# Transposing the normalised activations with DMAs in place of TensorE

## The chip, the cores and the metric

The kernel runs as one program on all 8 cores of one Trainium2 chip. Each core works on 4 of the 32 batch rows by itself; no core waits for another. The metric is the device time in microseconds of the slowest core.

## What is computed

A layer of a transformer on x of shape 32 x 2048 x 1024 in fp32: a layer norm, and then the sum of x, an attention branch and a feed-forward branch (FFN), both fed by the normalised x.

```
xn = layernorm(x)
# attention: 16 heads; q1,q2,k1,k2 = xn @ W (4 numbers per head)
L_q, L_k = normalised exterior products of (q1,q2) and (k1,k2)   # 6 numbers per head
scores   = L_q . J L_k * 6**-0.5, causal; attn = softmax(scores)
out_attn = (attn @ (xn @ W_v.T + b_v)) @ W_out.T + b_out          # 64 wide per head
# ffn: a complex 512x512 product, W_real and W_imag unfolded from small cores
out_real = x_real @ W_real.T - x_imag @ W_imag.T + bias_real
out_imag = x_real @ W_imag.T + x_imag @ W_real.T + bias_imag
y = x + out_attn + concat(out_real, out_imag)
```

## The kernel before

The engines' queues are written out by hand: each engine runs its instructions in the order of the program, and waits on semaphores (`t`, `v`, `s` for TensorE, VectorE and ScalarE, and one for each kind of DMA). SP (the sync engine) issues the loads and the small transfers, POOL the stores of y.

A core's batch has 2048 rows, in 16 tiles of 128. The work on a batch has these parts:

- A1 (lines 259 to 284) for each tile: SP loads 128 rows of x into `xstage` (line 261), VectorE takes the sums (lines 263 to 272), ScalarE the reciprocal of the deviation (lines 274 and 276), and VectorE writes the normalised rows into `xnstage` (line 281). There is one `xstage` and one `xnstage`; the load of the next tile waits until line 281 of this one is done.
- A2 (lines 286 to 300) for each tile: TensorE transposes the eight 128x128 blocks of `xnstage` into the PSUM banks F6 and F7 (line 294), and VectorE copies them out into `xnT` in bf16 (line 299), four blocks at a time.
- B1 and B2 (lines 303 to 373): queries and keys from `xnT`, in 4 chunks of 512 rows, through the same banks F6 and F7 (line 308 is B1's matmul, line 316 VectorE's copy of its result).
- V (from line 375): the values for each group of 4 heads (line 382).
- FFN (from line 397): the feed-forward branch for each tile, x loaded again into `x2stage` (line 400), which shares its memory with `xnstage`.
- Attention (`C_pair`): for each of 4 groups of heads (g), 2 pairs of heads (pr) and 4 windows of 512 queries (w), 4w + 4 steps over blocks of 128 keys: scores on TensorE (line 506), exponential on ScalarE (line 529), a mask on VectorE on the last four steps (line 537), and the product with V on TensorE into `O4` (line 546), whose 65th row collects the sums. A batch has 320 such steps.
- The division that ends a window (`emit_divide`): ScalarE forms the reciprocals with a logarithm and an exponential (lines 566 and 568), SP stores them to the DRAM scratch `rscr` (line 573) and, when they have landed, loads them back into `cdiv`, broadcast over 64 partitions (line 578), and VectorE multiplies `O4` into `oT` (line 584). `O4` has one buffer, so the next window's first product waits for line 584. Below, lines 573 and 578 are called the bounce.
- The output projection at the end of a batch (lines 455 to 468).

For batch 0 the parts A1 and A2 (16 tiles, one behind the other), B1, B2, V of one group and FFN run first, alone. For the later batches they are slipped into the attention of the batch before: `pace()` is called after each of the 320 steps and puts the next item into the queues when it is due, first A1 and A2 of each tile in turn, then FFN, and in the last group B1, B2 and V. The 16 tiles of A1 and A2 so fall into the first half of the steps, one tile every ten steps. The last batch has nothing to slip in.

Of the kernel before, what the change touches and what calls it, by code (L numbers as in the profile page):

```python
# [9 lines left out]
F32 = mybir.dt.float32  # L10
BF16 = mybir.dt.bfloat16
# [77 lines left out]
def mkap(sl, extra_offset, free_dims, nparts=None):  # L89
    p = list(sl.ap[0])  # L90
    if nparts is not None:
        p[1] = nparts
    return AP(sl.tensor, sl.offset + extra_offset, [p] + [list(d) for d in free_dims])


def pi_out_ap(tens):
    return mkap(tens, 0, [[512, 2], [1, 32], [32, 16]])


def build(nb=NB, debug=False):  # L100
# [27 lines left out]
    sb = lambda name, shape, dtype: st.enter_context(nc.sbuf_tensor(name, shape, dtype))  # L128
    with st:
        xnT = sb("xnT", [128, 8 * 2048], BF16)  # L130
# [10 lines left out]
        idt_sb = sb("idt", [128, 128], F32)  # L141
# [12 lines left out]
        fk_pad = sb("fkp", [128, 2048], BF16)  # L154
        exp_sb = sb("exps", [128, 2048], BF16)
        xstage = sb("xst", [128, 1024], F32)
        xnstage = sb("xnst", [128, 1024], F32)
        x2stage = xnstage
        ostage = sb("ost", [128, 2 * 1024], F32)
        cdiv = sb("cdiv", [64, 1024], F32)  # L160
        bscr = sb("bscr", [16, 512], F32)
# [6 lines left out]
        FB = [F6, F7]  # L168

        sems = {}  # L170
        for name in ["dwp", "dxp", "dws", "dyt", "dx", "dx2", "dyp", "dya", "dbo", "dbi", "t", "v", "s"]:
            sems[name] = Sem(st, nc, "sem_" + name)
        dwp, dxp, dws, dyt = sems["dwp"], sems["dxp"], sems["dws"], sems["dyt"]
        dx, dx2, dyp, dya = sems["dx"], sems["dx2"], sems["dyp"], sems["dya"]
        dbo, dbi = sems["dbo"], sems["dbi"]
        tS, vS, sS = sems["t"], sems["v"], sems["s"]
        TE, VE, SE, GE, SY = nc.tensor, nc.vector, nc.scalar, nc.gpsimd, nc.sync

# [30 lines left out]
        for ri in range(2):  # L209
            for mt in range(8):  # L210
                Fb = FB[mt % 2]
# [21 lines left out]
        for eng in (TE, VE, SE, SY, GE):  # L233
            dwp.wait(eng); dxp.wait(eng); dws.wait(eng)

        stx = {
            "xst_r": 0,
            "x2_r": 0,
            "xn_r": 0,
            "f_w": [0, 0],  # L240
            "f_r": [0, 0],
            "f_rs": [0, 0],
            "qk_w": 0,
            "xnT_tile": [0] * NT,
# [14 lines left out]
        def A1_tile(b1, tt):  # L259
            vS.wait(SY, stx["xst_r"])  # L260
            dx.inc(SY.dma_start(xstage[:], x_d[b1, tt * 128:(tt + 1) * 128, :]), 16)
            dx.wait(VE)
            vS.inc(VE.tensor_tensor(SCR[:, 0:1024], xstage[:], xstage[:], OP.mult))
            vS.inc(VE.reduce_sum(stat[:, 0:1], xstage[:], axis=AX.X))
            vS.wait(VE)
            vS.inc(VE.reduce_sum(stat[:, 1:2], SCR[:, 0:1024], axis=AX.X))
            vS.inc(VE.tensor_scalar(stat[:, 2:3], stat[:, 0:1], 1.0 / 1024, None, OP.mult))
            vS.wait(VE)
            vS.inc(VE.tensor_scalar(stat[:, 3:4], stat[:, 1:2], 1.0 / 1024, None, OP.mult))
            vS.inc(VE.tensor_tensor(stat[:, 4:5], stat[:, 2:3], stat[:, 2:3], OP.mult))  # L270
            vS.wait(VE)
            var_s = vS.inc(VE.tensor_tensor(stat[:, 5:6], stat[:, 3:4], stat[:, 4:5], OP.subtract))  # L272
            vS.wait(SE, var_s)
            sS.inc(SE.activation(stat[:, 6:7], stat[:, 5:6], AF.Ln, bias=cvec[:, 0:1]))  # L274
            sS.wait(SE)
            rstd_s = sS.inc(SE.activation(stat[:, 7:8], stat[:, 6:7], AF.Exp, scale=cvec[:, 2:3]))
            sS.wait(VE, rstd_s)
            vS.wait(VE)
            tS.wait(VE, stx["xn_r"])
            dx2.wait(VE)  # L280
            xn_s = vS.inc(VE.tensor_scalar(pi_out_ap(xnstage[:]), xstage[:], stat[:, 2:3],  # L281
                                           stat[:, 7:8], OP.subtract, OP.mult))
            stx["xst_r"] = xn_s
            stx["a_xn"] = xn_s

        def A2_tile(b1, tt):
            xn_s = stx["a_xn"]
            for half in range(2):
                Fb = FB[half]
                vS.wait(TE, max(xn_s, stx["f_r"][half]))  # L290
                sS.wait(TE, stx["f_rs"][half])
                for c4 in range(4):
                    c = half * 4 + c4
                    tS.inc(TE.transpose(Fb[:, c4 * 128:(c4 + 1) * 128],  # L294
                                        xnstage[:, c * 128:(c + 1) * 128], idt_sb[:]))
                stx["f_w"][half] = tS.n
                tS.wait(VE, stx["f_w"][half])
                out_ap = mkap(xnT[:], (half * 4) * 2048 + tt * 128, [[2048, 4], [1, 128]])
                stx["f_r"][half] = vS.inc(VE.tensor_copy(out_ap, Fb[:, 0:512]))  # L299
            stx["xn_r"] = tS.n  # L300
            stx["xnT_tile"][tt] = stx["f_r"][1]

        def B1_chunk(b1, ch):
            vS.wait(TE, max(stx["xnT_tile"][4 * ch + 3], stx["f_r"][0], stx["f_r"][1]))
            sS.wait(TE, max(stx["f_rs"][0], stx["f_rs"][1]))
            for mt in range(2):
                for kc in range(8):
                    ins = TE.matmul(FB[mt][:, 0:512],  # L308
                                    wqk_sb[:, kc * 256 + mt * 128: kc * 256 + mt * 128 + 128],
                                    xnT[:, kc * 2048 + ch * 512: kc * 2048 + ch * 512 + 512],  # L310
                                    start=(kc == 0), stop=(kc == 7))
                tS.inc(ins)
                stx["f_w"][mt] = tS.n
            for mt in range(2):
                tS.wait(VE, stx["f_w"][mt])
                stx["f_r"][mt] = vS.inc(VE.tensor_copy(QK_sb[:, mt * 512:(mt + 1) * 512],
                                                       FB[mt][:, 0:512]))
            stx["qk_w"] = vS.n
# [56 lines left out]
        def V_group(b1, g, cav_snap):  # L375
            for tt in range(NT):
                p = tt % 2
                Fb = FB[p]
                vS.wait(TE, max(stx["f_r"][p], stx["xnT_tile"][tt]))
                sS.wait(TE, stx["f_rs"][p])  # L380
                for kc in range(8):
                    ins = TE.matmul(Fb[:, 0:256],  # L382
                                    xnT[:, kc * 2048 + tt * 128: kc * 2048 + tt * 128 + 128],
                                    wv_sb[:, kc * 1024 + g * 256: kc * 1024 + g * 256 + 256],
                                    start=(kc == 0), stop=(kc == 7))
                tS.inc(ins)
                stx["f_w"][p] = tS.n
                tS.wait(VE, max(stx["f_w"][p], cav_snap))
                base = tt * 1040 + (4 * g) * 65
                vaug_ap = mkap(vaug[:], base, [[65, 4], [1, 64]])  # L390
                bvs = mkap(bv_bc[:], g * 256, [[64, 4], [1, 64]])
                vS.inc(VE.tensor_tensor(vaug_ap, Fb[:, 0:256], bvs, OP.add))  # L392
                ones_ap = mkap(vaug[:], base + 64, [[65, 4]])
                stx["f_r"][p] = vS.inc(VE.memset(ones_ap, 1.0))  # L394
            stx["vaug_grp"][g] = vS.n

        def FFN_pass1(b1, tt):
            vS.wait(SY, stx["x2_r"])
            tS.wait(SY, stx["xn_r"])
            dx2.inc(SY.dma_start(x2stage[:], x_d[b1, tt * 128:(tt + 1) * 128, :]), 16)  # L400
            dx2s = dx2.n
            vS.wait(TE, max(stx["f_r"][0], stx["f_r"][1], stx["xnT_tile"][tt]))
            sS.wait(TE, max(stx["f_rs"][0], stx["f_rs"][1]))
            tS.wait(VE, stx.get("neg_r", 0))
            for kc in range(4):
                vS.inc(VE.tensor_scalar(negscr[:, kc * 128:(kc + 1) * 128],  # L406
# [186 lines left out]
        for tt in range(NT):  # L593
            A1_tile(0, tt)
            A2_tile(0, tt)
        for ch in range(4):
            B1_chunk(0, ch)
            B2_chunk(0, ch, 0)
            B2_chunk(0, ch, 1)
# [7 lines left out]
        for b in range(nb):  # L607
            if b + 1 < nb:
                for tt in range(NT):
                    q1.append((0, lambda tt=tt, b1=b + 1: A1_tile(b1, tt)))  # L610
                    q1.append((1, lambda tt=tt, b1=b + 1: A2_tile(b1, tt)))
                for tt in range(NT):
                    q1.append((1, lambda tt=tt, b1=b + 1: FFN_pass1(b1, tt)))
                for ch in range(4):
                    q2.append((1, lambda ch=ch, b1=b + 1: B1_chunk(b1, ch)))
                    q2.append((1, lambda ch=ch, b1=b + 1: B2_chunk(b1, ch, 0)))
                    q2.append((1, lambda ch=ch, b1=b + 1: B2_chunk(b1, ch, 1)))
# [72 lines left out]
```

How the kernel before makes its waits and increments, by code:

```python
    def inc(self, instr, k=1):  # L81
        instr.then_inc(self.h, k)
        self.n += k
        return self.n
    def wait(self, eng, n=None):
        eng.wait_ge(self.h, self.n if n is None else n)
```

## Time and profile before

| | |
|---|---|
| median of 3 runs | 4830.19 us (4829.35 to 4843.36) |
| the profiled execution | 4842.17 us |
| its span, slowest core | 4841.1 us (cores 4794.0 to 4841.1) |
| TensorE matmul, VectorE, ScalarE busy | 59%, 29%, 30% of the span |
| mean granted TensorE clock | 0.659 |

The times of one table are of one execution. PE is TensorE's matmuls, PEld its weight loads, DVE is VectorE, ACT is ScalarE; SPq and POOLq are the DMA queues of SP and POOL. The granted clock is in parts of 2.4 GHz, so 0.50 is 1.2 GHz. The spans of matmuls are modelled and overlap.

### The profile page before, as it was taken

To read this page: it belongs to the slowest core of one execution; us is meant where nothing else is said; L and a number is where in the kernel's file an instruction comes from. 1 tells how busy PE (TensorE), PEld (TensorE's weight loads), DVE (VectorE), ACT (ScalarE), POOL (GpSimd) and SP (SyncE) were. 2 spreads that over 40 slices of the span, in tenths; PEclk is the share of its full clock that TensorE was granted. 3 is DMA by queue.
4 is the path that set the end of the run, shared out by engine and by line. 5 is a ranking of instruction groups with operands and counts; after the bars stand their busy time and mean duration, and the time that the engine had idled before them with its cause. 6 is when DMAs were issued, how large, how long until landed. Compare 5 with 4: busy or idle time off the path is not lost.

```text
span 4841.1 us, 35963 instructions; the slowest of 8 cores (4794.0 to 4841.1 us)
## 1 busy us (share of the span) xinstructions
PE 2859.6 (59%) x10528; PEld 979.4 (20%) x10528; DVE 1386.4 (29%) x2833; ACT 1475.1 (30%) x1729; POOL 129.5 (3%) x194
## 2 busy tenths in 40 slices
PE   1136755556665865556665685555665586666665
PEld 0112311112211421112111241111221151111112
DVE  0543443332222333332222233433222231111111
ACT  0000024443333014443333103444343203455550
POOL 2000000000000010000000000000000000000001
PEclk9986865557655875556665695556776696555558
DMA  6200210111100041011110031011120012000004
GB/s 77 47 31 1 93 66 27 33 38 61 66 27 11 5 72 33 27 33 57 61 48 7 9 57 37 29 33 42 61 70 13 5 30 47 14 14 11 14 11 72
DMA packets 88680, 180.26 MB, mean 37 GB/s; under 512 B 41760, under 2 KB 44968, under 8 KB 88496
## 3 DMA queue, kind: packets, MB, share of 16 engines
q0 software_dynamic: 55904, 73.28, 8.0%
q1 hardware_dynamic: 32592, 104.68, 7.3%
q8 instruction: 97, 1.59, 0.1%
q14 instruction: 87, 0.71, 0.0%
HBM read 114.36 MB, written 69.73 MB: 38 GB/s over the span
## 4 chain that ended last, share of the span: by engine, by line
PE 43%; DMA 22%; DVE 14%; ACT 12%; issue 8%; POOL 1%; DVEq 0%; SPq 0%; ACTq 0%; POOLq 0%
PE O L546 17%; DMA cdiv<-rscr 10%; DMA y<-ost 7%; PE S L506 7%; PE F L382 5%; ACT exps L529 5%; PE F L415 3%; DMA rscr<-cdiv 3%; ACT cdiv L568 3%; DVE oT L584 3%; ACT cdiv L566 3%; PE F L422 2%; PE F L308 2%; DVE exps L537 1%; DMA xst<-x 1%
## 5 line engine op out<-in xcount | busy, mean ns | idle before, releaser
L529 ACT ACTIVATE exps<-S 128x1024 bf16<-128x1024 f32 (+3 forms) x1280 | 1120.6, 893 | 2083.4 <-PE O L546 1352.0
L546 PE MATMUL O<-exps,vaug 128*65 128x512 bf16 (+3 forms) x2560 | 1043.6, 509 | 831.0 <-DVE oT L584 489.0
L506 PE MATMUL S<-fqp,fkp 6*128 6x512 bf16 (+3 forms) x2560 | 621.4, 494 | 427.6 <-ACT exps L529 421.0
L546 PEld LDWEIGHTS O<-exps,vaug 128*65 128x65 bf16 x2560 | 231.5, 136 | 1275.7 <-issue 1256.8
L584 DVE TENSOR_TENSOR oT<-O,cdiv 64x512 bf16<-64x512 f32 x256 | 174.8, 683 | 911.9 <-DMA cdiv<-rscr 904.3
L506 PEld LDWEIGHTS S<-fqp,fkp 6*128 6x128 bf16 x2560 | 141.2, 97 | 1149.1 <-issue 1142.9
L537 DVE TENSOR_TENSOR exps<-exps,tri 128x256 bf16<-128x256 bf16 x512 | 143.1, 290 | 737.3 <-ACT exps L529 734.8
L455 PE MATMUL S<-wout,oT 128*128 128x512 bf16 x1024 | 253.3, 408 | 91.4 <-DVE ost L464 81.9
L382 PE MATMUL F<-wv,xnT 128*128 128x256 bf16 x2048 | 245.8, 277 | 0.9 <-DVE vaug L394 0.7
L294 PE MATMUL F<-idt,xnst 128*128 128x128 f32 x512 | 121.3, 417 | 179.8 <-DVE xnst L281 179.8
L382 PEld LDWEIGHTS F<-wv,xnT 128*128 128x128 bf16 x2048 | 187.1, 99 | 64.7 <-issue 30.6
L566 ACT ACTIVATE cdiv<-O 1x1024 f32<-1x1024 f32 x128 | 130.1, 1016 | 150.1 <-PE O L546 150.1
L358 ACT ACTIVATE scr<-F,cvec 16x512 f32<-16x512 f32 x32 | 21.6, 674 | 500.1 <-PE F L356 500.1
L464 DVE COPY ost<-S 128x1024 f32<-128x1024 f32 x64 | 78.4, 1225 | 285.9 <-DMA y<-ost 256.2
L455 PEld LDWEIGHTS S<-wout,oT 128*128 128x128 bf16 x1024 | 102.9, 103 | 240.4 <-issue 144.5
L568 ACT ACTIVATE cdiv<-cdiv,cvec 1x1024 f32<-1x1024 f32 x128 | 146.8, 1147 | 11.8
L392 DVE TENSOR_TENSOR vaug<-F,bvbc 128x256 bf16<-128x256 f32 x256 | 109.3, 427 | 129.9 <-PE F L382 129.7
L294 PEld LDWEIGHTS F<-idt,xnst 128*128 128x128 f32 x512 | 103.6, 223 | 197.9 <-issue 196.8
L299 DVE CAST xnT<-F 128x512 bf16<-128x512 f32 x128 | 88.2, 691 | 176.9 <-PE F L294 176.5
L430 DVE TENSOR_TENSOR ost<-F,ballbc 128x512 f32<-128x512 f32 x64 | 44.3, 691 | 318.6 <-PE F L415 314.2
L415 PE MATMUL F<-wr,xnT 128*128 128x512 bf16 x256 | 104.6, 554 | 44.9 <-DVE negscr L406 44.9
L274 ACT ACTIVATE stat<-stat,cvec 128x1 f32<-128x1 f32 x64 | 18.8, 294 | 355.4 <-DVE stat L272 355.1
(71 smaller groups left out, 1951.5 us busy)
## 6 DMA issues: line engine op xcount, KB each, us to landing
y<-ost POOLq DMA_DIRECT2D x128, 512.0 KB, 5.1
xst<-x SPq DMA_DIRECT2D x64, 512.0 KB, 4.2
xnst<-x SPq DMA_DIRECT2D x64, 512.0 KB, 4.2
cdiv<-rscr SPq DMA_DIRECT2D x128, 256.0 KB, 3.6
wv<-wvT POOLq DMA_DIRECT2D x8, 256.0 KB, 18.6
wout<-woutT POOLq DMA_DIRECT2D x8, 256.0 KB, 19.3
tascr<-qk SPq DMA_DIRECT2D x16, 128.0 KB, 1.9
rscr<-cdiv SPq DMA_DIRECT2D x128, 4.0 KB
```

Of the source, the lines that this page charges most:

```text
L294: tS.inc(TE.transpose(Fb[:, c4 * 128:(c4 + 1) * 128], xnstage[:, c * 128:(c + 1) * 128], idt_sb[:]))
L382: ins = TE.matmul(Fb[:, 0:256], xnT[:, kc * 2048 + tt * 128: kc * 2048 + tt * 128 + 128], wv_sb[:, kc * 1024 + g * 256: kc * 1024 + g * 25 ...
L392: vS.inc(VE.tensor_tensor(vaug_ap, Fb[:, 0:256], bvs, OP.add))
L415: ins = TE.matmul(F6[:, 0:512], lhsT, rhs, start=(kc == 0), stop=(kc == 7))
L455: ins = TE.matmul(Pp[:, half * 512:half * 512 + 512], oT[:, pt * 2048 + tt * 128: pt * 2048 + tt * 128 + 128], wout_sb[:, pt * 1024 + half ...
L506: tS.inc(TE.matmul(S_ps[:, ss * 1024 + j * 512 + soff: ss * 1024 + j * 512 + 512], fk_pad[32 * m4:32 * m4 + 6, kt * 128:kt * 128 + 128], f ...
L529: sS.inc(SE.activation(e_out, e_in, AF.Exp))
L537: mk = vS.inc(VE.tensor_tensor(in0, in0, tri_b, OP.mult))
L546: ins = TE.matmul(O4[:, j * 512 + off:(j + 1) * 512], vaug[:, kt * 1040 + h * 65: kt * 1040 + h * 65 + 65], exp_sb[:, ss * 1024 + j * 512 ...
L566: sS.inc(SE.activation(cdiv[32:33, 0:1024], O4[64:65, 0:1024], AF.Ln))
L568: r_s = sS.inc(SE.activation(cdiv[0:1, 0:1024], cdiv[32:33, 0:1024], AF.Exp, scale=cvec[0:1, 3:4]))
L584: vS.inc(VE.tensor_tensor(oT[rr:rr + 64, pt * 2048 + w * 512: pt * 2048 + w * 512 + 512], O4[0:64, j * 512:j * 512 + 512], cdiv[0:64, j * ...
```

## The change

A2 no longer uses TensorE, PSUM or VectorE. `xnstage` becomes a bf16 tensor of its own, `x2stage` a separate fp32 one. When line 281 is done, SP issues eight DMAs per tile, each with `transpose=True`, which move one 128x128 block from `xnstage` straight into `xnT`. They count on a new semaphore `dtr`. What read `xnT` behind VectorE's semaphore now waits for `dtr`: B1, V and FFN on TensorE, and FFN's negation on VectorE; line 281 waits for the DMAs of the tile before. SP's wait for the transposes ahead of FFN's second load of x is gone.

```diff
-        xnstage = sb("xnst", [128, 1024], F32)
-        x2stage = xnstage
+        xnstage = sb("xnst", [128, 1024], BF16)
+        x2stage = sb("x2st", [128, 1024], F32)
...
-            tS.wait(VE, stx["xn_r"])
+            dtr.wait(VE, stx.get("xn_r_d", 0))
             dx2.wait(VE)
...
         def A2_tile(b1, tt):
             xn_s = stx["a_xn"]
-            for half in range(2):
-                Fb = FB[half]
-                vS.wait(TE, max(xn_s, stx["f_r"][half]))
-                sS.wait(TE, stx["f_rs"][half])
-                for c4 in range(4):
-                    c = half * 4 + c4
-                    tS.inc(TE.transpose(Fb[:, c4 * 128:(c4 + 1) * 128],
-                                        xnstage[:, c * 128:(c + 1) * 128], idt_sb[:]))
-                stx["f_w"][half] = tS.n
-                tS.wait(VE, stx["f_w"][half])
-                out_ap = mkap(xnT[:], (half * 4) * 2048 + tt * 128, [[2048, 4], [1, 128]])
-                stx["f_r"][half] = vS.inc(VE.tensor_copy(out_ap, Fb[:, 0:512]))
-            stx["xn_r"] = tS.n
-            stx["xnT_tile"][tt] = stx["f_r"][1]
+            vS.wait(SY, xn_s)
+            for c in range(8):
+                dtr.inc(SY.dma_start(xnT[:, c * 2048 + tt * 128: c * 2048 + tt * 128 + 128],
+                                     xnstage[:, c * 128:(c + 1) * 128], transpose=True), 16)
+            stx["xn_r_d"] = dtr.n
+            stx["xnT_tile"][tt] = dtr.n
 
         def B1_chunk(b1, ch):
-            vS.wait(TE, max(stx["xnT_tile"][4 * ch + 3], stx["f_r"][0], stx["f_r"][1]))
+            dtr.wait(TE, stx["xnT_tile"][4 * ch + 3])
+            vS.wait(TE, max(stx["f_r"][0], stx["f_r"][1]))
...
         def FFN_pass1(b1, tt):
             vS.wait(SY, stx["x2_r"])
-            tS.wait(SY, stx["xn_r"])
...
+            dtr.wait(VE, stx["xnT_tile"][tt])
             tS.wait(VE, stx.get("neg_r", 0))
```

## Rows read from the trace of the kernel before

**Rows 1.** The page: the span, and the chain that ended last, by line.
```profile
span 4841.1 us, 35963 instructions; the slowest of 8 cores (4794.0 to 4841.1 us)
...
PE O L546 17%; DMA cdiv<-rscr 10%; DMA y<-ost 7%; PE S L506 7%; PE F L382 5%; ACT exps L529 5%; PE F L415 3%; DMA rscr<-cdiv 3%; ACT cdiv L568 3%; DVE oT L584 3%; ACT cdiv L566 3%; PE F L422 2%; PE F L308 2%; DVE exps L537 1%; DMA xst<-x 1%
```

**Rows 2.** Timeline, first stage: start us, length us, engine, line; idle before.
```profile
146.24 1.27 DVE L281 TENSOR_SCALAR xnst<-xst,stat 128x1024 f32<-128x1024 f32 x1 [2.37 <-ACT stat L276]
...
147.76 1.94 PE L294 MATMUL F<-idt,xnst 128*128 128x128 f32 x8 [54.09 <-DVE xnst L281]
...
151.47 1.23 DVE L263 TENSOR_TENSOR scr<-xst 128x1024 f32<-128x1024 f32 x1 [0.97 <-DMA xst<-x]
...
301.07 1.27 DVE L281 TENSOR_SCALAR xnst<-xst,stat 128x1024 f32<-128x1024 f32 x1 [1.09 <-ACT stat L276]
```

**Rows 3.** Timeline around a tile at the end of a pair.
```profile
1022.56 1.26 DVE L281 TENSOR_SCALAR xnst<-xst,stat 128x1024 f32<-128x1024 f32 x1 [1.09 <-ACT stat L276]
...
1026.45 1.02 ACT L566 ACTIVATE cdiv<-O 1x1024 f32<-1x1024 f32 x1 [1.08 <-PE O L546]
...
1028.89 0.24 SPq L573 DMA_DIRECT2D rscr<-cdiv  x1
...
1033.99 1.40 DVE L584 TENSOR_TENSOR oT<-O,cdiv 64x512 bf16<-64x512 f32 x2 [5.11 <-DMA cdiv<-rscr]
...
1035.54 1.03 PE L546 MATMUL O<-exps,vaug 128*65 128x512 bf16 x2 [5.01 <-DVE oT L584]
```

**Rows 4.** Timeline around a tile in the middle of a pair.
```profile
1005.28 1.06 PE L546 MATMUL O<-exps,vaug 128*65 128x512 bf16 x2
...
1006.14 1.91 PE L294 MATMUL F<-idt,xnst 128*128 128x128 f32 x8
...
1008.52 1.06 PE L546 MATMUL O<-exps,vaug 128*65 128x512 bf16 x2
...
1010.05 1.06 PE L546 MATMUL O<-exps,vaug 128*65 128x512 bf16 x2
```

**Rows 5.** Windows behind two mid-pair tiles; the last batch: busy us, then PEclk.
```profile
694.30:695.30 1.00, 0.61 (x4) 0.24 (x4) 0.00 (x0) 1.00 (x2) 0.00 (x0) 1.00 0.00 0
...
3331.60:3332.60 1.00, 0.69 (x4) 0.14 (x2) 0.00 (x0) 1.00 (x2) 0.00 (x0) 1.00 0.00 0
4034.00:4741.00 707.00, 454.31 (x1322) 100.19 (x1323) 102.35 (x225) 352.23 (x384) 1.70 (x2) 0.50 0.05 14
```

**Rows 6.** Timeline of a mid-pair tile behind which the clock is 1.00.
```profile
690.77 1.91 PE L294 MATMUL F<-idt,xnst 128*128 128x128 f32 x8
...
709.11 1.02 ACT L566 ACTIVATE cdiv<-O 1x1024 f32<-1x1024 f32 x1 [1.44 <-PE O L546]
```

**Rows 7.** The copies of line 299 (ns min/median/max), and B1's first copy.
```profile
L299 DVE CAST xnT<-F x128: 680/692/693, 149.0 to 3330.1; 128x512 bf16<-128x512 f32 x128
...
309.29 0.69 DVE L316 COPY qk<-F 128x512 f32<-128x512 f32 x1 [3.93 <-PE F L308]
```

**Rows 8.** DMA issues: ns in the queue, min/median/max; KB and us to landing.
```profile
L573 SPq DMA_DIRECT2D rscr<-cdiv x128: 211/220/247, 657.4 to 4729.8; - x128
...
L261 SPq DMA_DIRECT2D xst<-x x64: 327/531/536, 135.8 to 3307.5; - x64
...
L224 SPq DMA_DIRECT2D tascr<-qk x16: 319/320/345, 25.6 to 94.3; - x16
L232 POOL DMA_DIRECT2D wr<-tascr x16: 780/818/855, 97.2 to 114.6; - x16
...
xst<-x SPq DMA_DIRECT2D x64, 512.0 KB, 4.2
...
tascr<-qk SPq DMA_DIRECT2D x16, 128.0 KB, 1.9
```

**Rows 9.** Timeline: a load of x behind a bounce, and its first use.
```profile
683.62 0.53 SPq L261 DMA_DIRECT2D xst<-x  x1
...
699.45 1.22 DVE L263 TENSOR_TENSOR scr<-xst 128x1024 f32<-128x1024 f32 x1
```

More of the change, by code:

```diff
@@ L170, in build @@
         sems = {}
-        for name in ["dwp", "dxp", "dws", "dyt", "dx", "dx2", "dyp", "dya", "dbo", "dbi", "t", "v", "s"]:
+        for name in ["dwp", "dxp", "dws", "dyt", "dx", "dx2", "dyp", "dya", "dbo", "dbi", "dtr", "t", "v", "s"]:
             sems[name] = Sem(st, nc, "sem_" + name)
@@ L175, in build @@
         dbo, dbi = sems["dbo"], sems["dbi"]
+        dtr = sems["dtr"]
         tS, vS, sS = sems["t"], sems["v"], sems["s"]
@@ L378, in V_group @@
                 Fb = FB[p]
-                vS.wait(TE, max(stx["f_r"][p], stx["xnT_tile"][tt]))
+                dtr.wait(TE, stx["xnT_tile"][tt])
+                vS.wait(TE, stx["f_r"][p])
                 sS.wait(TE, stx["f_rs"][p])
@@ L398, in FFN_pass1 @@
             vS.wait(SY, stx["x2_r"])
-            tS.wait(SY, stx["xn_r"])
             dx2.inc(SY.dma_start(x2stage[:], x_d[b1, tt * 128:(tt + 1) * 128, :]), 16)
             dx2s = dx2.n
-            vS.wait(TE, max(stx["f_r"][0], stx["f_r"][1], stx["xnT_tile"][tt]))
+            dtr.wait(TE, stx["xnT_tile"][tt])
+            vS.wait(TE, max(stx["f_r"][0], stx["f_r"][1]))
             sS.wait(TE, max(stx["f_rs"][0], stx["f_rs"][1]))
+            dtr.wait(VE, stx["xnT_tile"][tt])
             tS.wait(VE, stx.get("neg_r", 0))
```

## The prediction, written before the change was run

> **What bounds the kernel now.** I read the page first: the busy shares (TensorE 59% of the span, so no engine is the bound throughout), then the chain that ended last [rows 1]. It names what is: the two attention matmuls (lines 546 and 506), and next to them 10% for a transfer, the broadcast of the reciprocals back into cdiv. So I read each stage for the wait that ends last in it, and the change touches two stages.
>
> The first is the normalisation of batch 0, 16 tiles with nothing else running [rows 2]. xnstage of tile 0 is complete at 146.24 + 1.27 = 147.5 us. The transposes run on TensorE for 1.94 us from 147.76, and VectorE starts the next tile's squares at 151.47, when the load of x has landed. The last xn begins at 301.07, so a tile takes (301.07 - 146.24)/15 = 10.3 us. The ring is: xn done, load of x, statistics, xn. TensorE's transposes are beside that ring.
>
> The second is the attention of batches 0 to 2, in whose first half the 48 other tiles are slipped in. There are two kinds of place. Twenty-four tiles stand at the end of a pair, just ahead of a bounce of the reciprocals [rows 3]: xn ends at 1022.56 + 1.26 = 1023.8, ScalarE's logarithm starts at 1026.45, SP issues the store to rscr at 1028.89 (5.1 us after xn; 5.1 to 5.4 in all 24), VectorE divides at 1033.99, and TensorE goes on at 1035.54 after 5.01 us of idleness, because O4 has one buffer. Every microsecond by which SP issues the bounce later is one more of that idleness. The other 24 tiles stand in the middle of a pair, where TensorE has no gap [rows 4]: between two attention steps without a tile 10.05 - 8.52 = 1.53 us pass, and over the tile 1008.52 - 1005.28 = 3.24 us.
>
> **The change part by part.** *The 512 transposes on TensorE.* In the first stage and at the pair ends they cost nothing: there TensorE waits for the load or for the bounce. In the middle of a pair they cost 3.24 - 1.53 = 1.71 us, 24 times: 41.0 us saved.
>
> *What goes with them: the clock.* After the mid-pair tile at 690.77 the granted clock is 1.00 (2.4 GHz) at 694 to 695; the same reading 3.5 us after each of the 24 mid-pair tiles gives 1.00 at 16 and 0.50 at 8 [rows 5], the first and the last of them. In the last batch, which has no tiles slipped in, the clock is 0.50 for all of 707 us. So the rises come behind the transposes. One is worth, from the tile to the logarithm that ends its pair, (1026.45 - 1006.14) - (709.11 - 690.77) = 20.31 - 18.34 = 1.97 us [rows 3, 4, 6]. If all 16 go: 31.5 us lost. Net of both: 41.0 - 31.5 = 9.5 us saved. The Trainium skill (TensorE: Matmul & The Clock Gate, Part 4: PE-mode transpose) says that transpose-mode work does not count as busy for the clock gate in the way matmuls do; by that the 16 rises would stay and the saving would be 41.0. The readings of the last batch speak against it, so the trace decides here, and I keep 9.5.
>
> *The 128 copies out of PSUM (line 299) and xnstage in bf16.* VectorE's two copies per tile, 692 ns each [rows 7], lie inside the wait for the load (first stage) or while VectorE has nothing due (attention). I cost them at nothing; without that cover they would be 64 x 1.4 = 89 us. The conversion to bf16 happens in line 281; its input stays fp32, and I leave its 1.25 us as it is. The separate x2stage removes one wait of SP before the first FFN load, which is early anyway: nothing.
>
> *B1 starts early.* TensorE no longer has 16 transposing tiles in its queue ahead of the first chunk of B1, and may run that chunk while tiles are still being normalised. VectorE now takes its result at 309.29 [rows 7]; it can take it right behind the last xn, 301.07 + 1.27 = 302.3. Saved: 6.9 us, once.
>
> *512 transposing DMAs on SP.* This is the term that decides. Let t be the time that one takes out of SP's queue, so 8t per tile. No DMA of this kind is in the trace. From below: SP spends 0.22 us on the one-row store to rscr and 0.53 us on the 512 KB load of x [rows 8]. From above: if they leave one at a time, the nearest row is the 128 KB store of 128 rows to tascr, 1.9 us from issue to landing. A transposing DMA is no plain copy: each source row of 256 bytes is spread over 128 partitions, and the trace has one DMA that cuts its data into pieces that small, line 232 (1024 pieces of 16 elements), which costs its queue 0.78 to 0.82 us without any transposing. The value should lie over that and under 1.9; I take t = 1.2, near the middle between 0.53 and 1.9. So 8t = 9.6 us.
>
> Where does it fall? (a) First stage: SP has the load of x for the next tile behind the eight DMAs, so the ring gets longer by 8t, for 15 tiles: 15 x 9.6 = 144 us. (b) The 24 pair-end tiles: SP can start on the DMAs when xn is done, and the bounce is due 5.1 us later: 24 x (9.6 - 5.1) = 108 us more idleness of TensorE. (c) Twelve mid-pair tiles have their bounce 13.2 us or more after xn: 9.6 fits, nothing. (d) The other twelve come in SP's order just behind a bounce, and ahead of the load of x for the next tile [rows 9]: that load is issued at 683.62 and its data are first used at 699.45. With 9.6 more and 4.2 to land it is there at 697.4; nothing.
>
> Sum: 144.0 + 108.0 - 9.5 - 6.9 = +235.6 us. The profiled execution took 4842.2 us (span 4841.1 and 1.1 around it); the sum against it gives 5077.8. The median of the three runs is 4830.2, 12 us below, so I forecast 5066.
>
> The Trainium skill (VectorE: DVE Perf Modes, The three transpose paths) gives 1309 ns for a 128x128 bf16 transpose through the DMA crossbar, 390 ns on TensorE, and advises TensorE when PSUM will do. No row here shows the DMA; for TensorE the trace has 1.94/8 = 0.24 us. With 1309 ns the sum would be 15 x 10.5 + 24 x 5.4 - 16.4 = +271, an estimate from that page.
>
> **The rivals.**
> (R1, the forecast, 45%) t about 1.2: +236. Its own range, t from 1.0 to 1.45: +176 to +322, so 5006 to 5152.
> (R2, 30%) The DMAs cost SP what plain ones of 128 rows do, t 0.32 to 0.53: at 0.53 8t is 4.2 us, under 5.1, so the bounces stay unharmed; 15 x 4.24 - 16.4 = +47, 4877. At 0.32: +22, 4852. For it speaks that SP's rows hardly grow with the work; against it, that none of them transposes. The Trainium skill (Advanced Engine Details and Errata, X-Bar Transpose) says that transpose DMAs are as fast as regular ones, which would be this case; no run here shows it yet.
> (R3, 13%) They go one at a time, t = 1.9, 8t = 15.2: 15 x 15.2 = 228; 24 x 10.1 = 242; and in (d) the load lands at 683.5 + 15.2 + 4.2 = 702.9 against 699.45, 12 x 3.5 = 41 us of stalled statistics, masks behind them. Together +495, 5325. Against it: DMAs of one queue overlap elsewhere.
> (R4, faster, 6%) The freed TensorE decides. The rises of the clock stay without the transposes (41.0 saved), B1 gives 6.9, and SP pays only its smallest row: 15 x 1.76 = 26. Then 26.4 - 47.9 = -21, 4809. It needs t under 47.9/120 = 0.40 and the rises kept; the last batch at 0.50 throughout speaks against it.
> (R5, 6%) Between R2 and R4, no more than 14.5 us either way: t about 0.2 to 0.25 with the rises lost, or 0.3 to 0.5 with them kept.
>
> **How the numbers follow.** What this kernel's measurement can tell from no change is about 0.3%, 14.5 us. R1, R2 and R3 are slower: 88%, and the edge of R5 makes it 89; within 0.3% 5; faster 6. The predicted time is R1's. The range must take in R2 at 0.53 and go up between R1 and R3: 4860 to 5300. It leaves out the lowest part of R2, R4, R5 and most of R3, about 2 in 10.
>
> **What would show it.** In the first stage, the distance between two xn of neighbouring tiles should be 10.3 + 8t: 20 us by R1, 14.5 by R2, 25 by R3; that row gives t directly. SP's rows for the eight DMAs give t again. At the pair ends, the time from xn to the store to rscr should be 8t or 5.1, whichever is longer, and TensorE's wait for the division should grow by the rest. In mid-pair, the step over a tile should be 1.53 us and the clock should stay at 0.50 to the end of the tiles' half. VectorE's first copy of B1 should stand right behind the last xn. The prediction is wrong if 8t stays under 5.1 (the bounces untouched), if the transposed rows land so late that TensorE waits for them, or if the DMAs' traffic slows the reload of cdiv itself, which I have at nothing.

## The result and the profile after

The changed kernel took 5161.83 us (median of 8 runs, 5156.08 to 5184.11) against 4837.63 us of the kernel before (8 runs, 4829.35 to 4846.96): the ratio is 1.0676, with a 95% interval of 1.0658 to 1.0695. It is slower by 324 us. I had forecast 5066, 236 us more; the way and the range held, the size was too small by 88 us. In some executions, whatever the kernel, the cores of one die or of both show a granted clock lower by 0.01 or 0.02 and take longer by about 1%, which is why the medians of two runs below, 4950 and 4933 us, lie above their fastest executions, 4923 and 4912 us.

The page of the changed kernel, of its slowest core (span, busy line, the chain by line, and the DMA issues with KB and us to landing):

```profile
span 5159.2 us, 35339 instructions; the slowest of 8 cores (5134.5 to 5159.2 us)
...
PE O L542 16%; DMA cdiv<-rscr 9%; SPq L291 7%; DMA y<-ost 7%; PE S L502 7%; PE F L377 5%; DMA rscr<-cdiv 3%; PE F L411 3%; ACT exps L525 3%; DVE oT L580 3%; ACT cdiv L564 2%; PE F L418 2%; DVE xnst L282 2%; ACT cdiv L562 2%; PE F L302 1%
...
L282 DVE TENSOR_SCALAR xnst<-xst,stat 128x1024 bf16<-128x1024 f32 x64 | 167.3, 2615 | 122.5 <-ACT stat L277 108.7
...
xnT<-xnst SPq DMA_TRANSPOSE x512, 2.3
```

Against [rows 1] there are two newcomers in the chain: SP's queue on line 291, the transposing DMAs, with 7%, and VectorE's line 282, the normalisation, with 2%. The group line of 282 shows why: one takes 2615 ns. It took 1254 ns before.

From here on all rows are of core 0 in both kernels (span 4841.1 before, 5150.5 after), so that the same core is compared. The timeline of the changed kernel at a tile at the end of a pair answers to [rows 3]. (A "pair end" is the end of one call of `C_pair`, which is one window of one pair of heads. The tiles stand at the steps 4, 14, 24 and 34 of each 40, and windows end at the steps 4, 12, 24 and 40: so every second tile, 24 in all, stands just ahead of a bounce.)

```profile
1243.67 2.57 DVE L282 TENSOR_SCALAR xnst<-xst,stat 128x1024 bf16<-128x1024 f32 x1 [1.09 <-ACT stat L277]
...
1246.32 10.02 SPq L291 DMA_TRANSPOSE xnT<-xnst  x8
...
1250.00 1.15 ACT L564 ACTIVATE cdiv<-cdiv,cvec 1x1024 f32<-1x1024 f32 x1
...
1256.55 0.27 SPq L569 DMA_DIRECT2D rscr<-cdiv  x1
...
1261.69 1.40 DVE L580 TENSOR_TENSOR oT<-O,cdiv 64x512 bf16<-64x512 f32 x2 [13.49 <-DMA cdiv<-rscr]
...
1263.23 1.03 PE L542 MATMUL O<-exps,vaug 128*65 128x512 bf16 x2 [10.28 <-DVE oT L580]
```

ScalarE has the reciprocals ready at 1251.15, but SP issues the store at 1256.55, when its eight DMAs are out. TensorE's wait grew from 5.01 to 10.28 us. The reload of `cdiv` itself is no slower: it lands in 3.6 us in both kernels.

Two of TensorE's waits grew, each summed over the whole core (us, times, longest). The first is for the division. The second is for the mask (line 537 before, 533 after), which stands behind the normalisation in VectorE's order. The changed kernel, then the kernel before:

```profile
PE O L542 <- DVE oT L580: 604.9, 96, 11.7
PE O L542 <- DVE exps L533: 352.1, 274, 7.7
...
PE O L546 <- DVE oT L584: 489.0, 96, 6.7
PE O L546 <- DVE exps L537: 305.1, 270, 6.3
```

That is 115.9 us more for the division and 47.0 us more for the mask.

SP's time for one DMA, in ns (min, median, max):

```profile
L291 SPq DMA_TRANSPOSE xnT<-xnst x512: 1093/1232/2375, 147.5 to 3647.8; - x171
```

And the busy times in four stretches, from the end of the first xn to the end of the sixteenth in the first stage, and the same in each of the three batches that have tiles slipped in (busy us of PE, PEld, DVE, ACT, POOL; then the granted clock):

```profile
147.40:480.80 333.40, 6.25 (x16) 2.09 (x16) 99.55 (x122) 8.82 (x30) 0.00 (x0) 0.63 0.14 36
827.30:1275.20 447.90, 208.42 (x612) 47.42 (x612) 138.31 (x217) 172.53 (x211) 0.00 (x0) 0.50 0.13 36
2009.30:2458.80 449.50, 208.35 (x612) 47.40 (x612) 138.55 (x217) 172.47 (x211) 0.00 (x0) 0.50 0.13 36
3191.90:3639.00 447.10, 208.46 (x612) 47.42 (x612) 138.36 (x218) 172.56 (x211) 0.00 (x0) 0.50 0.13 36
```

The same four of the kernel before:

```profile
147.50:302.30 154.80, 29.11 (x120) 23.53 (x120) 99.69 (x151) 8.82 (x30) 0.00 (x0) 1.00 0.15 51
652.30:1046.10 393.80, 217.57 (x728) 69.79 (x728) 138.73 (x247) 170.90 (x210) 0.00 (x0) 0.55 0.10 31
1787.50:2180.40 392.90, 211.78 (x728) 69.26 (x728) 138.69 (x248) 170.56 (x210) 0.00 (x0) 0.57 0.10 31
2926.60:3324.00 397.40, 220.19 (x728) 70.15 (x728) 138.79 (x248) 170.96 (x210) 0.00 (x0) 0.54 0.10 30
```

These eight rows are the account. The first stage goes at 333.4/15 = 22.2 us per tile against 10.3: 178.6 us more. The three stretches of the attention take 448.2 us in the mean against 394.7: 160.4 us more in all. Between the first stage and the first tile of the attention, 302.3 to 652.3 became 480.8 to 827.3, 3.5 us less. The rest of the program took 26 us less. Most of it lies in the two stretches between those with tiles: 741 and 746 us before, 734 and 733 after. The change touches them only in FFN's waits and in the memory of `x2stage`. They take 728 to 739 us in the first ten runs below, in which `x2stage` is a tensor of its own, but 732 and 725 us in the comparison at the end, in which it is not; the cause of the 26 us is not shown. 178.6 + 160.4 - 3.5 - 26.1 = 309.4, the difference of the two spans of core 0. And the clock: it is 0.50 in all three stretches with tiles, where it was 0.54 to 0.57.

### The profile page after: what moved, and what is told of

It reads as the page before. It is cut to its first block, busy times and chain, and to the rows that moved or that the text cites. A ratio compares the mean times of both kernels' runs of the same rounds, so it can differ in the third digit from the quotient of the medians.

```text
span 5159.2 us, 35339 instructions; the slowest of 8 cores (5134.5 to 5159.2 us)
## 1 busy us (share of the span) xinstructions
PE 2784.6 (54%) x10016; PEld 879.7 (17%) x10016; DVE 1385.5 (27%) x2705; ACT 1478.4 (29%) x1729; POOL 129.5 (3%) x194
## 4 chain that ended last, share of the span: by engine, by line
PE 40%; DMA 21%; DVE 14%; ACT 9%; issue 8%; SPq 8%; POOL 0%; DVEq 0%; ACTq 0%; POOLq 0%
PE O L542 16%; DMA cdiv<-rscr 9%; SPq L291 7%; DMA y<-ost 7%; PE S L502 7%; PE F L377 5%; DMA rscr<-cdiv 3%; PE F L411 3%; ACT exps L525 3%; DVE oT L580 3%; ACT cdiv L564 2%; PE F L418 2%; DVE xnst L282 2%; ACT cdiv L562 2%; PE F L302 1%
## 5 line engine op out<-in xcount | busy, mean ns | idle before, releaser
L542 PE MATMUL O<-exps,vaug 128*65 128x512 bf16 (+3 forms) x2560 | 1077.6, 523 | 997.7 <-DVE oT L580 613.1
L502 PE MATMUL S<-fqp,fkp 6*128 6x512 bf16 (+3 forms) x2560 | 636.6, 506 | 452.7 <-ACT exps L525 446.1
L282 DVE TENSOR_SCALAR xnst<-xst,stat 128x1024 bf16<-128x1024 f32 x64 | 167.3, 2615 | 122.5 <-ACT stat L277 108.7
L324 PE MATMUL F<-qk,perm 64*96 64x512 f32 x64 | 55.5, 962 | 262.8 <-DVE qk L310 255.0
L302 PE MATMUL F<-xnT,wqk 128*128 128x512 bf16 x256 | 85.3, 507 | 141.2 <-DMA xnT<-xnst 134.6
L264 DVE TENSOR_TENSOR scr<-xst 128x1024 f32<-128x1024 f32 x64 | 78.2, 1222 | 257.4 <-DMA xst<-x 257.0
```

The source lines that it names most:

```text
L502: tS.inc(TE.matmul(S_ps[:, ss * 1024 + j * 512 + soff: ss * 1024 + j * 512 + 512], fk_pad[32 * m4:32 * m4 + 6, kt * 128:kt * 128 + 128], f ...
L542: ins = TE.matmul(O4[:, j * 512 + off:(j + 1) * 512], vaug[:, kt * 1040 + h * 65: kt * 1040 + h * 65 + 65], exp_sb[:, ss * 1024 + j * 512 ...
```

## The experiments

All ratios are to the kernel before, run beside it on the same chip. Its median was 4822 to 4862 us on the chips used, so runs are compared by their ratios and not by their times. The profile rows are of one execution each. "Stretches" are the three stretches of the attention with tiles slipped in, of core 0: 394.7 us in the mean before, 448.2 after.

### Half of the DMAs

```diff
-            for c in range(8):
+            for c in range(0, 8, 2):
                 dtr.inc(SY.dma_start(xnT[...], xnstage[...], transpose=True), 16)
```

> The changed kernel with only four of the eight transposing DMAs per tile (every second block of xnT is left at zero). Theory Q (SP's queue is held 1.25 us by each DMA): 4 DMAs hold it 5.05 us instead of 10.1, so the first stage loses 15 x 5.05 = 76 us, and at the 24 pair ends the bounce is due about 4.9 us after xn and is almost untouched, 24 x 5.2 = 125 us gone: about 4960 us. Rival L (what is late is the landing of the last DMA, not the queue): the landing of one DMA stays, so under 30 us are gained. Rival C (the clock without the transposes on TensorE makes the attention long): the first stage gives 76 and the attention nothing, about 5085 us.

This run and the one with halves of blocks also clear `xnT` once ahead of the first stage. Measured: 4977.3 us, ratio 1.0277 (1.0250 to 1.0305), near the 4960 us foreseen. The first stage went at 256.3/15 = 17.1 us per tile, 5.1 less; the first of the stretches:

```profile
740.00:1150.80 410.80, 208.33 (x612) 47.33 (x612) 138.45 (x217) 172.50 (x211) 0.00 (x0) 0.50 0.13 34
```

It is 37 us shorter than with eight (38 in the mean of the three), and its clock is the same 0.50. TensorE's waits for the division are 489.9 us, what they were before the change (489.0). A DMA still takes 2.3 us to land. So the cause of both terms is the number of DMAs in the queue, and rivals L and C fall. That it is not the amount they move is shown by the two sizes of DMA below.

### TensorE's side alone

```diff
         def A2_tile(b1, tt):
             xn_s = stx["a_xn"]
+            if b1 > 0:
+                stx["xnT_tile"][tt] = xn_s
+                return
```

> The kernel before with x2stage as a tensor of its own, and with A2 left out (no transposes, no copies) for the 48 tiles in the attention; xnT keeps the rows of batch 0. It is the TensorE side of the change alone. My term: 41.0 us of mid-pair work gone, 31.5 us of risen clock gone with it: -9.5 us, about 4828, and the granted clock 0.50 in all of the tiles' stretches. Rival (the rises have another cause and stay): -41 us, about 4797, and the clock in these stretches as before, 0.55.

`x2stage` is a tensor of its own here too. Measured: 4832.46 us, ratio 0.9975 (0.9959 to 0.9992), that is 4 to 20 us less. The three stretches:

```profile
647.10:1037.30 390.20, 206.94 (x608) 47.06 (x608) 117.82 (x217) 171.60 (x210) 0.00 (x0) 0.50 0.10 31
1768.80:2163.00 394.20, 207.01 (x608) 47.08 (x608) 117.97 (x218) 171.65 (x210) 0.00 (x0) 0.50 0.10 30
2898.80:3288.60 389.80, 207.01 (x608) 47.04 (x608) 117.91 (x217) 171.62 (x210) 0.00 (x0) 0.50 0.10 31
```

Together 1174.2 us against 1184.1: 9.9 us gained, where I had 9.5. That the two come so close is luck, since the three stretches of one kernel differ by 4 us among themselves. Without the transposes TensorE is busy 5 to 13 us less in each stretch, and with them goes every rise of the clock. VectorE's busy time fell by 21 us per stretch, the copies, and nothing came of it. The rival (41 us, a ratio of 0.9915) falls.

### The transposes back on TensorE, for nothing

The changed kernel with, at each tile of the attention:

```diff
+            if b1 > 0:
+                for half in range(2):
+                    ...
+                    for c4 in range(4):
+                        tS.inc(TE.transpose(FB[half][:, c4 * 128:(c4 + 1) * 128],
+                                            idt_sb[:], idt_sb[:]))
```

> The changed kernel, and on TensorE again eight fp32 transposes at each of the 48 tiles in the attention, of the identity, whose results nobody reads. If the transposes raise the clock: rises are back behind the mid-pair ones, the mean clock of the tiles' stretches goes from 0.50 to about 0.55, and the time changes by +41 - 31 = +10 us, about 5172. If they don't: the clock stays 0.50 and the time goes up by 41 us, about 5203.

Measured: 5173.36 us, ratio 1.0679 (1.0652 to 1.0706), against 1.0676 without them. The first two stretches:

```profile
823.40:1278.40 455.00, 220.09 (x732) 70.09 (x732) 138.31 (x217) 171.71 (x211) 0.00 (x0) 0.54 0.13 35
2008.90:2459.30 450.40, 214.66 (x732) 69.44 (x732) 138.64 (x217) 171.49 (x211) 0.00 (x0) 0.56 0.13 36
```

The clock is back at 0.54 and 0.56, and the stretches take 453.6 us in the mean, 5.4 more than without. That is 16 us in all, where I had 10. So 24 transposing gaps of 1.71 us cost far less than 41 us: with them comes the clock. The mechanism of this term is shown from both sides. What it is in the transposes that raises the clock, and whether other work of the same length would, no run tested.

### The scattered bf16 write

```diff
-VE.tensor_scalar(pi_out_ap(xnstage[:]), xstage[:], ...)
+VE.tensor_scalar(mkap(xnstage[:], 0, [[512, 2], [32, 16], [1, 32]]),
+                 mkap(xstage[:], 0, [[512, 2], [1, 16], [16, 32]]), ...)
```

> The changed kernel; line 282 reads xstage with the stride of the permutation and writes xnstage in one contiguous run, the same numbers in the same places. Theory W (the scattered bf16 write makes it 2.6 us instead of 1.25): it falls to about 1.25, the first stage gets 16 x 1.35 = 22 us shorter and the attention up to 48 x 1.35 = 65: 5075 to 5110 us. Rival (the conversion to bf16 itself, or any stride, costs it): it stays near 2.6 and the time at 5162.

The diff names the two patterns; the buffers, the numbers and their places are the same. Measured: 5094.9 us, ratio 1.0520 (1.0488 to 1.0553), within what was foreseen. The row of the instruction (ns, min, median, max):

```profile
L282 DVE TENSOR_SCALAR xnst<-xst,stat x64: 1136/1142/1209, 140.3 to 3567.5; 128x1024 bf16<-128x1024 f32 x64
```

The same row of the changed kernel:

```profile
L282 DVE TENSOR_SCALAR xnst<-xst,stat x64: 2508/2596/2765, 144.7 to 3636.3; 128x1024 bf16<-128x1024 f32 x64
```

Both convert fp32 to bf16, so the conversion is not what makes it long; it is the write of single bf16 elements 64 bytes apart that doubles the instruction. (The fp32 write before had the same stride in elements, 128 bytes; whether the spacing or the size of the element matters was not separated.) TensorE's wait for the mask shows how it reaches the time. It is back at what it was before the change, 305.1:

```profile
PE O L543 <- DVE exps L534: 304.1, 273, 6.4
```

The stretches went from 448.2 to 432.1 us (48 us in all), the first stage from 22.2 to 20.6 us per tile (24 us): 72 us of the kernel, a term that my sum did not have.

### The load of x first

```diff
             vS.wait(SY, xn_s)
+            if tt + 1 < NT:
+                load_x(b1, tt + 1)
             for c in range(8):
```

> The changed kernel, with the load of x for the next tile issued ahead of the eight DMAs. Theory Q: in the first stage the load leaves the ring behind the DMAs; what is left is the one xnstage, free when the last DMA has landed: 0.5 + 10.1 + 2.3 and then 2.6 for line 282, about 15.5 us per tile instead of 22.2, 15 x 6.7 = 100 us gained; at the pair ends the bounce stands behind one load more, 24 x 0.5 = 12 us lost: about 5074. Rival (the landing is hidden as well, the queue alone counts): 12.7 us per tile, about 5030. Rival (the DMAs slow the load beside them): less than 50 us gained.

Measured: 5075.04 us, ratio 1.0435 (1.0418 to 1.0453). The timeline of the first stage:

```profile
148.92 10.10 SPq L297 DMA_TRANSPOSE xnT<-xnst  x8
152.26 1.23 DVE L268 TENSOR_TENSOR scr<-xst 128x1024 f32<-128x1024 f32 x1 [3.86 <-DMA xst<-x]
...
160.29 2.65 DVE L286 TENSOR_SCALAR xnst<-xst,stat 128x1024 bf16<-128x1024 f32 x1 [3.70 <-DMA xnT<-xnst]
```

The load now runs beside the DMAs and lands as fast as before, and a new wait closes the ring: xnstage has one buffer, and VectorE waits 3.70 us until the last DMA has read and landed. 14.5 us per tile, where I had 15.5: the 2.3 us to landing begin at a DMA's issue, so the sum counted the last DMA's own 1.23 us twice. The stretches grew by 3.3 us (8 x 0.5 = 4 expected). Both rivals fall: the landing is waited for (3.70 us), and 115 us are gained in the first stage.

### The DMAs behind the bounce

```diff
+        def A2_held(b1, tt):        # in place of A2_tile, in the attention
+            if stx["left"] == 0:    # last step of a window
+                stx["held"] = [lambda: A2_tile(b1, tt)]
+            else:
+                A2_tile(b1, tt)
...
             stx["pending_div"]()    # the bounce
...
+            for fn in stx.get("held", []):
+                fn()
```

> The changed kernel, with the DMAs of the 24 pair-end tiles put into SP's queue behind the bounce instead of ahead of it. Theory Q: TensorE's wait there is back from 10.3 to 5.0 us, 24 x 5.2 = 125 us gained, about 5037. Rival C (the clock, or the DMAs' traffic beside the reload of cdiv, makes the attention long): less than 40 us gained, since the traffic then runs just beside the reload.

Measured: 5135.43 us, ratio 1.0558 (1.0530 to 1.0586). That is 57 us gained and not 125. The stretches take 434.6 us, 13.6 less each where I expected 42. TensorE's waits for the division are back where they were, so the bounce is free:

```profile
PE O L552 <- DVE oT L590: 478.1, 96, 6.5
```

Something else was late. The timeline of the same kernel:

```profile
1246.28 10.12 SPq L291 DMA_TRANSPOSE xnT<-xnst  x8
...
1256.50 0.53 SPq L262 DMA_DIRECT2D xst<-x  x1
...
1260.28 1.22 DVE L264 TENSOR_TENSOR scr<-xst 128x1024 f32<-128x1024 f32 x1 [9.64 <-DMA xst<-x]
...
1264.70 0.29 ACT L275 ACTIVATE stat<-stat,cvec 128x1 f32<-128x1 f32 x1 [5.63 <-DVE stat L273]
...
1265.29 1.92 ACT L535 ACTIVATE exps<-S 128x1024 bf16<-128x1024 f32 x2
```

The load of x for the next tile is behind the DMAs, so VectorE waits 9.64 us for it, and ScalarE, which has the tile's small logarithm in its order between two exponentials, waits 5.63 us for VectorE. The exponentials, and TensorE with them, stand still. A wait was exchanged for another. The next run tests this.

### Both: behind the bounce, and the load first

> The DMAs of pair-end tiles behind the bounce, and the load of x ahead of them, at every tile; one xnstage, the scattered write kept. If what was missing in the run with the bounce alone is the load of x behind the DMAs (its data come late for the statistics, and ScalarE's two small operations hold up its exponentials), the tiles' stretches of the attention fall by about 42 us each against the changed kernel, from 448 to about 406: some 75 us above the kernel before in all, ratio 1.015. Rival (DMA traffic beside the reload of cdiv, or the clock): they stay at about 434 us, ratio 1.03.

Measured: 4950.36 us, ratio 1.0213 (1.0169 to 1.0258). The stretches are 407.7, 405.4 and 407.2 us, as expected, and the first stage goes at 14.5 us per tile. The rival, 434 us, falls. The median is above the 1.015 that I wrote, which lies under its interval; but the execution whose trace is read took 4922.56 us, a ratio of 1.016. The other three took 4945 to 4972 us. So the stages account for the one execution that was traced, and the excess of the median does not come from them.

### Two sizes of DMA

Eight DMAs of half a block:

```diff
-dtr.inc(SY.dma_start(xnT[:, o: o + 128], xnstage[:, c * 128:(c + 1) * 128], transpose=True), 16)
+dtr.inc(SY.dma_start(xnT[:, o: o + 64], xnstage[0:64, c * 128:(c + 1) * 128], transpose=True), 16)
```

> The changed kernel with eight DMAs per tile, each transposing only 64 of the 128 rows of its block (the other half of xnT is left at zero). If SP's time goes by the amount that is transposed, one takes about 0.65 us, and the kernel falls to that of the run with four DMAs, ratio about 1.03. If it goes by the instruction, one takes 1.25 us as before and the ratio stays at 1.067.

And one of eight blocks:

```diff
-            for c in range(8):
-                dtr.inc(...)
+            dtr.inc(SY.dma_start(mkap(xnT[:], tt * 128, [[2048, 8], [1, 128]]),
+                                 xnstage[:], transpose=True), 16)
```

> The changed kernel with one DMA per tile, whose destination walks the eight blocks, in place of eight DMAs. If SP's time goes by the instruction, it holds the queue for 1.3 to 1.6 us per tile: the first stage loses 8.7 us per tile and the pair ends their 5.2, ratio about 1.012. If it goes by the amount that is transposed, one row of about 9 to 10 us stands where eight stood, and the ratio is 1.06 to 1.067.

Measured: 5170.09 us for the halves, ratio 1.0673 (1.0644 to 1.0701), and 4932.93 us for the one, ratio 1.0180 (1.0136 to 1.0223). SP's row for the halves:

```profile
L292 SPq DMA_TRANSPOSE xnT<-xnst x512: 1088/1228/2353, 143.0 to 3650.3; - x171
```

and for the one:

```profile
L290 SPq DMA_TRANSPOSE xnT<-xnst x64: 1232/1242/1991, 141.0 to 3380.8; - x64
```

64 rows, 128 rows and 8 x 128 rows all cost SP 1.23 to 1.24 us. The time goes by the instruction; only the landing grows, from 2.3 to 3.1 us. With one DMA SP is held 1.24 us per tile, TensorE's waits for the division are back at 488.6 us (the stretches take 407.7 us), and the first stage goes at 13.5 us per tile. I had written 1.012 for the one, which lies under its interval. Two of its four executions, 4912 and 4918 us, are at 1.014 and 1.015. The stages gained what was foreseen, 130 and 121 us, and 5162 less those is 4910: the 1.012 was too low by itself.

### The mends together

> The changed kernel with the three mends together and two xnstage buffers (two semaphores): load first, DMAs of pair-end tiles behind the bounce, strided read and contiguous write. If the three terms are all there is, the first stage goes at 10.7 to 11.3 us per tile against 10.3 before, B1 gives about 5 us and mid-pair 9.5: 4810 to 4850 us, no different from the kernel before. If something else of the DMAs costs, it stays above 4880.

Besides the three mends this run has two buffers for `xnstage`, so that VectorE need not wait for the landing. Measured: 4831.0 us against 4861.58, ratio 0.9933 (0.9919 to 0.9947). The 4810 to 4850 us foreseen are a ratio of 0.994 to 1.003 to the 4837.63 us of the kernel before in the result; it came out just under that. It still has eight DMAs per tile. The first stage goes at 161.3/15 = 10.75 us per tile, and the stretches take 390.5 us, 4.2 less than before the change. So no cost of the DMAs is left over besides the terms named: their queue time and where it stands, the one buffer, and the scattered write. It beats the kernel before by 0.7%.

Last, one DMA per tile, the contiguous write and x loaded two tiles ahead; and, for comparison, the kernel before with the loads ahead and nothing else:

```diff
+        def load_x(b1, tt):         # two buffers, a semaphore for each
+            vS.wait(SY, stx["xst_r"][tt % 2])
+            stx["dx_n"][tt % 2] = dxs[tt % 2].inc(SY.dma_start(xst2[...], x_d[...]), 16)
...
             xn_s = stx["a_xn"]
+            if tt + 2 < NT:
+                load_x(b1, tt + 2)
```

> One transposing DMA per tile, the strided read with the contiguous write, and x loaded two tiles ahead into two buffers. SP is then held 1.24 us per tile, VectorE has no copies, and the load is off the ring: the first stage should go at VectorE's own 6.6 + 1.2 = 7.8 us per tile against 10.3 before (38 us gained), the attention's stretches at 390 us against 394.7 (13 us), B1 and its surroundings 9 to 12 us: about 60 us under the kernel before, ratio 0.987. If the DMA's landing (3.1 us) or SP holds the ring, it stays at 10.5 us per tile and the ratio at 0.993.

> The kernel before, with only the two buffers for x, loaded two tiles ahead; transposes on TensorE. If VectorE's in-order copies out of PSUM (3.0 us from xn to the end of the second copy) then close the ring, the first stage goes at 9.7 us per tile, 10 us gained: ratio 0.998. If the loads were all that held it, 7.8 us per tile and ratio 0.992.

Measured: 4744.64 us for the first, ratio 0.9833 (0.9808 to 0.9857), and 4793.29 us for the second, ratio 0.9934 (0.9915 to 0.9954). The first stage and the first of the stretches of the former:

```profile
139.90:237.90 98.00, 5.74 (x16) 2.00 (x16) 75.96 (x121) 8.82 (x30) 0.00 (x0) 0.67 0.51 115
576.20:963.10 386.90, 206.83 (x608) 47.05 (x608) 117.50 (x218) 171.47 (x210) 0.00 (x0) 0.50 0.16 40
```

In this run `xnstage` shares the memory of `x2stage` again. Its first stage goes at 6.5 us per tile. I had written 7.8, and had counted line 282 twice: the 6.6 us of the kernel before, from the square at 151.47 in [rows 2] to the end of the xn below, 158.11, contain it.

```profile
156.89 1.22 DVE L281 TENSOR_SCALAR xnst<-xst,stat 128x1024 f32<-128x1024 f32 x1 [1.09 <-ACT stat L276]
```

Now VectorE's own order nearly fills the ring, but the landing of the one DMA ends at the same moment: behind the loads it takes 4.5 us in the median and not 3.1, and in the first stage it ended the wait before xn in 12 of 15 tiles (us, times, longest):

```profile
DVE x2st L292 <- DMA xnT<-x2st: 13.7, 12, 1.5
```

In the comparison the first stage goes at 144.3/15 = 9.6 us per tile, as expected, because VectorE waits in order for TensorE's transposes and copies them. The DMA form is worth 3.1 us per tile here, since it takes these copies out of VectorE's order. That is 46 us of the 49 between the two kernels, whose intervals do not touch: with the loads ahead and one instruction per tile, the DMAs beat TensorE's transposes by 1%. The comparison's gain, 29 us where I had 10, is more than the 10 us of its first stage; two of its stretches came out at 385.3 and 384.8 us, and why the early loads help there was not tested.

## Why the prediction was right, and where it was too small

**The number.** The range of 4860 to 5300 us held, but it was made to take in the rivals R2 and, in part, R3. R1's own range, t from 1.0 to 1.45, was added up wrong: it gives +173 to +314 and not +176 to +322, and the +324 measured lies above either. The mechanism of R1 was right; its size was not.

**What bounds the kernel.** Right. Both places that I named, the ring of the first stage and the bounce at the 24 pair ends, are where the time went, 178.6 and the larger part of 160.4 us.

**t, SP's time per DMA.** I took 1.2 us; the row shows 1.232, and 10.1 us for eight with the gaps. The choice near the middle between 0.53 and 1.9 had no row behind it, and that it landed so close is luck. The Trainium skill (VectorE: DVE Perf Modes, The three transpose paths) has 1309 ns for a 128x128 bf16 transpose by DMA; the trace's 1232 ns in SP's queue is near it, though the run with halves (1228 ns) shows that the size of the block has nothing to do with it. The Trainium skill (Advanced Engine Details and Errata, X-Bar Transpose) has transpose DMAs as fast as regular ones; here one costs SP 1.23 us where a plain load of 128 rows costs 0.53, so for SP's queue the measurement decides against it. For the landing the trace agrees: eight blocks, 256 KB, in one DMA land in 3.1 us, the plain reload of `cdiv`, 256 KB too, in 3.6.

**(a) The first stage.** 144 forecast, 178.6 measured. The DMAs are 15 x 10.1 = 152. Of the other 27 the scattered write has 24 (the run with the strided read).

**(b) The pair ends.** 108 forecast; TensorE's waits for the division grew by 115.9. Without the DMAs the bounce would have been due 5.1 us behind xn, as forecast: xn ends at 1246.24, ScalarE is done at 1251.15, and [rows 3] has the same store about 0.2 us after that. SP issued it 10.3 us behind xn. With 10.1 us for the eight in place of 9.6 my sum gives 120.

**(c) and (d).** Nothing forecast. The run with the DMAs behind the bounce shows how close (d) is to the edge: there the same order at the pair ends cost about 3.5 us each (42 - 13.6 = 28 us per stretch, over 8). At the twelve places of (d) the next tile's statistics are due later: in the changed kernel one such load is issued at 1231.84 and first used at 1238.26, and loads land in 4.1 us.

**Mid-pair and the clock.** -9.5 forecast, -9.9 measured with TensorE's side alone, and the counter-test gives the clock back. The step over a mid-pair tile, whose DMAs SP issues from 919.08 on, is 1.53 us as forecast:

```profile
919.29 1.06 PE L542 MATMUL O<-exps,vaug 128*65 128x512 bf16 x2
...
920.82 1.06 PE L542 MATMUL O<-exps,vaug 128*65 128x512 bf16 x2
```

The sentence of the Trainium skill (TensorE: Matmul & The Clock Gate, Part 4: PE-mode transpose), by which transposes would not count as busy in the same way, does not fit this kernel: without them no rise is left in these stretches, and with idle ones of the identity the mean clock is 0.54 and 0.56 again. Whether these fp32 transposes run in the mode that the sentence means, no run shows.

**B1 early.** -6.9 forecast, -3.5 measured up to the first tile of the attention, which itself has the longer line 282. VectorE's copy does start right behind the last xn, at 480.35; the half that is missing is not explained.

**The step that failed: "its input stays fp32, and I leave its 1.25 us as it is".** Line 282 takes 2.6 us, because its output, not its input, changed: bf16 elements written 64 bytes apart. 1.35 us more, 64 times (86 us), of which 72 us reached the time: 24 in the ring of the first stage, and 48 in the attention, where the mask stands behind it. With it the forecast would have been 236 + 72 = 308 us. I priced the edit by the operand that stayed and not by the one that the diff changed. Nor did I bound it: the trace before has no bf16 write with such a stride, and the range of the sum should have had an end for it.

In the trace of core 0 the three places of the forecast took 99.9 us more than their terms (34.6 in the first stage, 61.9 in the stretches, 3.4 around B1). The write has 72 of it, the longer t 7.5 in the first stage and 7.9 at the pair ends; some 12 us, those around B1 among them, have no cause shown. Against them stand the 26 us that the rest of the program took less, on which I had no term.

## What to carry to other kernels

A DMA that takes over an engine's work is priced by the queue that issues it, and by what is behind it in that queue: here the 10 us would have been free in the attention, had the load of x and the bounce stood ahead of them, and nearly free in the first stage with a second buffer and the contiguous write besides. Before you move such transfers, ask first whether one instruction can do them all; eight in one saved about as much as both reorderings together (1.0180 and 1.0213, whose intervals overlap), with a smaller edit. Whether another engine's queue could have taken them was not tested. And when a diff changes the type of a strided operand, price that instruction anew, by the side that changed.

## What the runs showed of the hardware

- A transposing DMA costs SP's queue 1.23 us for 64 rows, 1.23 us for 128 rows and 1.24 us for eight blocks of 128x128 in one instruction, whose landing takes 3.1 us against 2.3 (4.5 us with a 512 KB load of x issued just ahead of it).
- VectorE's fp32 to bf16 pass over 128x1024 takes 2.6 us when it writes single elements 64 bytes apart and 1.14 us when it reads fp32 with that stride and writes without one. In fp32 the scattered write took 1.25 us.
- Eight fp32 transposes slipped into the attention are followed at 16 of 24 mid-pair places by a granted clock of 1.00 in place of 0.50, while the attention's own matmuls stayed at 0.50 in all 707 us of the last batch [rows 5]. Of the 41 us that they cost, all but 10 to 16 come back.
